# Store order of a mixture-of-experts stage: first and second picks alternate from quad to quad

## The reference

```python
h = gelu(ri @ r1_w.T + r1_b); probs = softmax(h @ r2_w.T)        # ri: the token and five statistics of it
topp, topi = top_k(probs, 2)                                     # each token picks two experts
score = where(routed, probs, -inf)
idx = argsort(-score, axis=0)[:cap].T                            # each of 32 experts takes its best 160 tokens
xe = xf[idx]
hact = silu(gate) * upv                                          # from xe @ w_up[e]
ye = hact @ w_down[e]
out = zeros((T, C)).at[idx.reshape(-1)].add(w * ye)              # the scatter-add: a token gets 0, 1 or 2 addends
out = out + sum_g gw * adapter_g(xf)                             # 16 small adapters, each shared by two experts
x = x + 0.5 * out
```

## Time and profile before

| | us |
|---|---|
| median of 3 runs | 1718.28 (1717.09 to 1720.53) |
| the profiled execution, its own time | 1708.64 |
| its span, first to last instruction | 1706.9 |
| first dispatch, POOL's first gather to its last store landed | 780.7 to 1101.5 |
| second dispatch, the same | 1385.5 to 1706.9 |
| mean granted TensorE clock | 0.905 of full speed |

### The profile page before, as it was taken

How to read it: one execution, slowest core, us unless ns; L and a number is a source line. 1 busy time by engine, 2 the same in 40 slices (tenths; PEclk the granted TensorE clock), 3 DMA queues, 4 the chain that set the end, 5 groups by cost and what they waited for, 6 DMA issues and landing times. The chain is left out here.

```text
span 1706.9 us, 26203 instructions
## 1 busy us (share of the span) xinstructions
PE 1427.4 (84%) x9328; PEld 1073.3 (63%) x9328; DVE 986.2 (58%) x2856; ACT 690.4 (40%) x1640; POOL 560.4 (33%) x465
## 2 busy tenths in 40 slices
PE   6899889999999678546999999299995459999994
PEld 5567545565555455335988999176663349888993
DVE  8787777787876479685552212057766855521110
ACT  4222137666666467443522332013333425323221
POOL 6522210000000154124254754332211232637644
PEclk9989889999999989656999999689997569999997
DMA  3035463423220013413687996421113326879983
GB/s 109 19 118 151 115 123 67 91 37 87 47 55 3 1 62 113 159 37 108 212 233 226 241 316 169 77 92 50 41 47 113 109 63 198 268 211 261 265 230 41
DMA packets 113483, 211.95 MB, mean 124 GB/s; under 512 B 20069, under 2 KB 79370, under 8 KB 104138
## 3 DMA queue, kind: packets, MB, share of 16 engines
q1 hardware_dynamic: 87338, 178.93, 32.7%
q0 software_dynamic: 26016, 31.34, 11.8%
HBM read 158.71 MB, written 51.12 MB: 123 GB/s over the span
## 5 line engine op out<-in xcount | busy, mean ns | idle before, releaser
L952 DVE TENSOR_REDUCE attnm_top<-psum 128x1 f32<-128x384 f32 (+3 forms) x384 | 212.9, 598 | 59.0 <-PE psum L1037 54.9
L1174 ACT ACTIVATE attnm_prob<-psum 128x512 f32<-128x512 f32 (+1 forms) x384 | 192.1, 530 | 88.9 <-PE psum L1047 82.3
L2553 DVE SCALAR_TENSOR_TENSOR moe2e_h<-moe2e_gate,psum 128x160 f32<-128x160 f32 x160 | 50.6, 321 | 187.2 <-ACT moe2e_gate L2491 187.1
L2553 DVE SCALAR_TENSOR_TENSOR moe1e_h<-moe1e_gate,psum 128x160 f32<-128x160 f32 x160 | 50.6, 321 | 186.3 <-ACT moe1e_gate L2491 186.2
L2356 POOL DMA_INDIRECT out<-moe2e_y,moe_scatter_i x74 | 116.4, 1573 | 113.8 <-DMA out<-moe2e_y,moe_scatter_i 58.4
L2356 POOL DMA_INDIRECT x_sum<-moe1e_y,moe_scatter_i x74 | 115.6, 1562 | 112.3 <-DMA x_sum<-moe1e_y,moe_scatter_i 65.9
L2425 PE MATMUL psum<-moe1e_xgT,moe_w_up 128*128 128x160 f32 x1024 | 149.5, 304 | 0.8 <-issue 0.8
L2425 PE MATMUL psum<-moe2e_xgT,moe_w_up 128*128 128x160 f32 x1024 | 149.4, 303 | 0.8 <-issue 0.8
L2425 PEld LDWEIGHTS psum<-moe1e_xgT,moe_w_up 128*128 128x128 f32 x1024 | 144.5, 193 | 3.5 <-issue 2.5
L2425 PEld LDWEIGHTS psum<-moe2e_xgT,moe_w_up 128*128 128x128 f32 x1024 | 144.3, 193 | 3.4 <-issue 2.5
L1348 POOL DMA_INDIRECT moe_xg<-xn_rows,moe_gather_i x80 | 83.4, 1043 | 155.0 <-DVE moe_gather_i L1537 93.0
(11 more groups left out here) (420 smaller groups left out, 3100.7 us busy)
## 6 DMA issues: line engine op xcount, KB each, us to landing
moe_w_up<-in_expert_up SPq DMA_DIRECT2D x64, 1024.0 KB, 8.4
moe_w_down<-in_expert_down SPq DMA_DIRECT2D x64, 512.0 KB, 6.9
attnm_q_hat<-q_parts SPq DMA_DIRECT2D x72, 128.0 KB, 4.6
moe_a_up<-in_adapter_up SPq DMA_DIRECT2D x32, 256.0 KB, 9.4
q_parts<-attnf_q_part SPq DMA_DIRECT2D x12, 512.0 KB, 2.8
attnm_k_hat<-k_parts SPq DMA_DIRECT2D x72, 64.0 KB, 2.3
x_res<-in_x SPq DMA_DIRECT2D x8, 512.0 KB, 8.9
v_tails<-attnf_v_tail SPq DMA_DIRECT2D x4, 1024.0 KB, 5.3
```

Source lines behind the costliest of these rows:

```text
L952: nc.vector.tensor_reduce(top[:, n // QUADS % 2, tiles[0]:tiles[-1] + 1, hh:hh + 1], s.ps[:, u.bank, 0:len(tiles) * width].rearrange("p (t ...
L1174: nc.scalar.activation(prob[:, i % NPROB, at:GROUP], s.ps[:, u.bank, at:GROUP], ACT.Exp).then_inc(taken[u.bank], 1)
L2553: nc.vector.scalar_tensor_tensor(out=h[:, HELD[n], i, :], in0=gate[:, i, :], scalar=1.0 if i < INTER // P else SCALE_A, in1=s.ps[:, u.bank ...
```

## The change

1. The waits of the stores are split: `y_out` becomes four semaphores, one for each parity of the quad and each list.
2. Quads 0 to 5: an even quad stores its first list and then its second, an odd quad the second and then the first. So the list that a quad begins with is the one that the quad before ended with, and as no token has two second picks (or two first ones), these may be in flight together. The wait for the quad before, and the return of its `y` buffer, move from ahead of the quad's first store to behind its third. The tail is stored ahead of tile 3.
3. Quads 6 and 7 are written out as six phases with a wait behind each. `whole` and `of_any` go.
4. The spare rows are doubled, so that neighbouring quads don't share any: `spare_no` is made by two iotas and a copy of 40 columns instead of 5, and the output has 640 more rows.

Gathers, loads and the order of all other engines stay.

```diff
--- before.py
+++ after.py
@@ -1203,7 +1203,7 @@
 ST_TILES = EQ * CAP // P
 SLOT_TILES = SLOTS // P
 ROW = C + 16
-SPARE = ST_TILES * P
+SPARE = 2 * ST_TILES * P
 QUADS_E = EXPERTS // EQ
 VALUES = 2
 HALF = EXPERTS // 2
@@ -1247,8 +1247,12 @@
             chain.link(nc.gpsimd.iota(ints[:, at:at + n], pattern, base=base, channel_multiplier=step))
             chain.link(nc.gpsimd.tensor_copy(out[:], ints[:, at:at + n]))
             at += n
-        chain.link(nc.gpsimd.iota(ints[:, at:at + ST_TILES], [[P, ST_TILES]], base=TOKENS + 1, channel_multiplier=1))
-        chain.link(nc.gpsimd.tensor_copy(s.spare_no[:], ints[:, at:at + ST_TILES]))
+        many = QUADS_E // 2 * 2 * ST_TILES
+        for n in range(QUADS_E // 4):
+            first = n * many // (QUADS_E // 4)
+            chain.link(nc.gpsimd.iota(ints[:, first:first + 4 * ST_TILES], [[ST_TILES * P, 2], [0, 2], [P, ST_TILES]], base=TOKENS + 1,
+                                      channel_multiplier=1))
+        chain.link(nc.gpsimd.tensor_copy(s.spare_no[:], ints[:, 0:many]))
         chain.link(nc.gpsimd.tensor_copy(self.mine[:, 0:HALF], s.ident[:, 0:HALF]))
         for j in range(1, PARTS):
             chain.link(nc.gpsimd.tensor_tensor(self.mine[:, 0:HALF], self.mine[:, 0:HALF], s.ident[:, HALF * j:HALF * (j + 1)], ALU.add))
@@ -1290,7 +1294,7 @@
     s.e_down = sb("e_down", [P, EXPERTS], F32)
     s.tile_no = sb("tile_no", [P, 2 * TILES], F32)
     s.row_no = sb("row_no", [P, 1], F32)
-    s.spare_no = sb("spare_no", [P, ST_TILES], F32)
+    s.spare_no = sb("spare_no", [P, QUADS_E // 2 * 2 * ST_TILES], F32)
     s.same_e = sb("same_e", [P, P], F32)
     s.before_e = sb("before_e", [P, P], F32)
     s.same_b = sb("same_b", [P, P], BF16)
@@ -1391,7 +1395,6 @@
         self.held = sb("held", [P, VALUES, self.tiles])
         self.token = sb("token", [P, self.tiles])
         self.added, self.spare = (sb(n, [P, self.quads, 2, ST_TILES]) for n in ("added", "spare"))
-        self.of_any, self.whole = sb("of_any", [P, self.quads, ST_TILES]), sb("whole", [P, self.quads, ST_TILES], I32)
         (self.scored, self.score_turned, self.score_copied, self.halved, self.high_made, self.low_made, self.tried, self.parted,
          self.counted, self.signed, self.totaled, self.tied, self.offset, self.placed, self.place_turned, self.pos_made,
          self.valued, self.hot_made, self.slotted, self.copied, self.listed, self.rows_known, self.slots_made, self.dve) = (
@@ -1538,15 +1541,9 @@
         nc.vector.tensor_scalar(first, second, -1.0, 1.0, ALU.mult, ALU.add)
         chain.link(nc.vector.tensor_tensor(added[:, :, 1], of_quad, second, ALU.mult))
         chain.link(nc.vector.tensor_tensor(added[:, :, 0], of_quad, added[:, :, 1], ALU.subtract))
-        spare_no = s.spare_no[:].rearrange("p (o k) -> p o k", o=1).broadcast_to([P, self.quads, ST_TILES])
-        chain.link(nc.vector.scalar_tensor_tensor(out=self.of_any[:], in0=of_quad, scalar=0.0, in1=spare_no,
-                                                  op0=ALU.is_equal, op1=ALU.mult))
-        nc.vector.scalar_tensor_tensor(out=self.whole[:], in0=of_quad, scalar=-1.0, in1=self.of_any[:],
-                                       op0=ALU.add, op1=ALU.add)
-        spare_no = s.spare_no[:].rearrange("p (o k) -> p o k", o=1).broadcast_to([P, 2 * self.quads, ST_TILES])
         chain.link(nc.vector.scalar_tensor_tensor(
-            out=spare[:].rearrange("p q i k -> p (q i) k"), in0=added[:].rearrange("p q i k -> p (q i) k"), scalar=0.0,
-            in1=spare_no, op0=ALU.is_equal, op1=ALU.mult))
+            out=spare[:].rearrange("p q i k -> p (q i k)"), in0=added[:].rearrange("p q i k -> p (q i k)"), scalar=0.0,
+            in1=s.spare_no[:], op0=ALU.is_equal, op1=ALU.mult))
         nc.vector.scalar_tensor_tensor(
             out=scatter_i, in0=added[:].rearrange("p q i k -> p (q i k)"), scalar=-1.0,
             in1=spare[:].rearrange("p q i k -> p (q i k)"), op0=ALU.add, op1=ALU.add).then_inc(self.slots_made, 1)
@@ -2217,7 +2214,7 @@
     gate = sb("gate", [P, PAIRS, CAP])
     HELD = [0, 1, 2, 3, 4, 0, 1, 2]
     h = sb("h", [P, EQ + 1, PAIRS, CAP])
-    y_out = sem("y_out")
+    y_out = [[sem(f"y_out{q}_{i}") for i in range(2)] for q in range(2)]
     y_free = [sem(f"y_free{q}") for q in range(2)]
     silu, chosen, weighed = sem("silu"), sem("chosen"), sem("weighed")
     banks = Banks(st)
@@ -2339,61 +2336,56 @@
                 pool.wait_ge(chosen, quad - 1)
             m.gather(pool, quad)
 
-        stored = itertools.count(1)
-
-        def add(quad):
-
+        stored = collections.Counter()
+
+        def store(quad, i, tiles):
 
             q, t = quad % 2, quad // 2
-            choice, at = m.choices[quad // late.quads], quad % late.quads
-            whole = [choice.whole[:, at, k:k + 1] for k in range(EQ)]
-            first, second = ([scatter_i[:, (quad * 2 + i) * ST_TILES + k:(quad * 2 + i) * ST_TILES + k + 1]
-                              for k in range(ST_TILES)] for i in range(2))
-
-            def store(k, rows):
+            for k in tiles:
                 u = u_tails[q] if k == TAIL else u_down[EQ * q + k]
+                at = (quad * 2 + i) * ST_TILES + k
                 pool.wait_ge(taken[u.bank], u.after(t))
-                nc.gpsimd.indirect_dma_start(total, bass.IndirectOffsetOnAxis(ap=rows, axis=0),
+                nc.gpsimd.indirect_dma_start(total, bass.IndirectOffsetOnAxis(ap=scatter_i[:, at:at + 1], axis=0),
                                              y[:, q, k, :], None, bounds_check=TOKENS + SPARE - 1, oob_is_err=True,
-                                             compute_op=ALU.add).then_inc(y_out, 16)
-                return next(stored)
-
-            def landed(n):
-                if n > 0:
-                    pool.wait_ge(y_out, 16 * n)
-
-            done = add.done
-            landed(done)
-            if quad > 0:
-                pool.sem_inc(y_free[1 - q], 1)
-            if quad < QUADS_E - 1:
-                for rows in (first, second):
-                    for k in range(ST_TILES):
-                        done = store(k, rows[k])
-                    if rows is first:
-                        landed(done)
-            else:
-                for k in range(EQ - 1):
-                    done = store(k, whole[k])
-                    landed(done)
-                for rows in (first, second):
-                    for k in (TAIL, EQ - 1):
-                        done = store(k, rows[k])
-                    if rows is first:
-                        landed(done)
-            add.done = done
-
-        add.done = 0
+                                             compute_op=ALU.add).then_inc(y_out[q][i], 16)
+                stored[q, i] += 1
+
+        def landed(quad, i):
+            pool.wait_ge(y_out[quad % 2][i], 16 * stored[quad % 2, i])
+
         gather(1)
         late.lows(pool)
         pool.wait_ge(x_kept, 16 * GROUPS)
-        for quad in range(QUADS_E):
+        for quad in range(QUADS_E - 2):
+            one, other = (0, 1) if quad % 2 == 0 else (1, 0)
             if quad + 2 == QUADS_E // 2:
                 pool.wait_ge(late.slots_made, 1)
-            if quad + 2 < QUADS_E:
-                gather(quad + 2)
-            add(quad)
-        pool.wait_ge(y_out, 16 * add.done)
+            gather(quad + 2)
+            store(quad, one, range(EQ - 1))
+            if quad > 0:
+                landed(quad - 1, one)
+                pool.sem_inc(y_free[1 - quad % 2], 1)
+            store(quad, one, (TAIL, EQ - 1))
+            landed(quad, one)
+            store(quad, other, range(ST_TILES))
+
+        a, b = QUADS_E - 2, QUADS_E - 1
+        store(a, 0, (0, 1))
+        landed(a - 1, 0)
+        pool.sem_inc(y_free[1], 1)
+        landed(a, 0)
+        store(a, 1, (0, 1))
+        landed(a, 1)
+        store(a, 0, (2, TAIL, 3))
+        landed(a, 0)
+        store(a, 1, (2, TAIL, 3))
+        store(b, 1, (0, 1))
+        landed(a, 1)
+        landed(b, 1)
+        store(b, 0, (0, 1, 2, TAIL, 3))
+        landed(b, 0)
+        store(b, 1, (2, TAIL, 3))
+        landed(b, 1)
 
     def tensor(pe):
         def turn_x(t, q, i):
```

## The result

The changed kernel took 1705.24 us (median of 4 runs, 1701.92 to 1708.93) against 1719.32 us for the kernel before (4 runs, 1717.09 to 1720.53): a ratio of 0.9915 [0.9889, 0.9940], 14.1 us less. The forecast was 1708.3, in 1702.5 to 1714.0. Two later sets of runs, on two chips, gave 1696.37 against 1709.01 (0.9927 [0.9905, 0.9948]) and 1696.27 against 1706.77 (0.9941 [0.9923, 0.9960]), so 12.6 and 10.5 us less.

The account below looks back on a forecast made before the run. POOL's stores and landing waits behind PE's last result were taken to bound the end. Savings of 5.15 + 4.8 us in the two dispatches, 10.0 together, off the median 1718.28 gave 1708.3 us, range 1702.5 to 1714.

Parts of the forecast that it names:

- What bounds the kernel: Behind PE's last result, POOL's stores and landings set the end: tails of 24.6 and 25.4 us can shorten.
- The sum of the tail: From quad 5's last store to the last store: 35.7 us of stores plus 18.6 of waits, 54.3.
- w1: Landing wait behind quad 6's first two stores, two stores after quad 5's five: 4.4 us, from 2.9 to 6.85.
- w2: Landing wait behind the second phase's two stores, issued as the down loads go out: 4.7 us, from 2.9 to 7.6.
- w3: Landing wait behind the third phase's three stores, issued as the loads end: 3.5 us, from 2.9 to 6.9.
- w4: Landing wait behind the fourth phase's five stores, on idle DMA engines: 3.0 us.
- w5: Landing wait behind the fifth phase's five stores, on idle DMA engines: 3.0 us.
- the forecast's own signs: Profile signs: bursts of 2, 2, 3, 5, 5, 3, waits near 4.4, 4.7, 3.5, 3.0, 3.0, last landing 5 us closer to PE's end.
- Small phases land as if idle: Rival in the tail: two-store phases slip in ahead of the loads, saving 7.5 + 0.5 per dispatch, 1702 us; chance 0.18.
- The second phase waits out the whole down load: Rival in the tail: its two stores land only after the loads, wait 11.9 us, 3.4 lost, 1721.7 us; chance 0.10.
- Quads 0 to 5: Savings on POOL ahead of the tail, from one wait and the lists: 0.5 us per dispatch, bounds 0 and 0.7.
- The later buffer return: `y_free` comes 5.6 us later, taken as 0; rival: ACT's stalls reach PE, half the saving goes, 1713 us; chance 0.12.

Follow-up runs that it names:

- the alternation alone: Against the kernel before: alternating list order with later buffer return in quads 0 to 6, last quad stored as before; 1704.2 us, ratio 0.9964.
- the two experiments on it: Against the changed kernel: buffer return ahead of the quad's first stores (1699.74 us), or behind all five stores of its first list (1698.51 us).

## Why the prediction was right

**What bounds the kernel**: right. The gain is on POOL, behind PE's last result; that result did not move but for the first profile (294.2 to 297.3 in the later two, 294.8 to 297.1 in the two of before), and the last landing came closer to it.

**The sum of the tail**: right in its total. Over the three profiles of the change, six tails, the means are

| | w1 | w2 | w3 | w4 | w5 | tail |
|---|---|---|---|---|---|---|
| forecast | 4.4 | 4.7 | 3.5 | 3.0 | 3.0 | 54.3 |
| measured, mean of six | 3.9 | 4.6 | 4.3 | 3.1 | 3.0 | 54.7 |
| lowest to highest | 2.7–4.7 | 2.9–7.5 | 2.9–8.6 | 2.9–4.0 | 2.8–3.1 | 52.0–58.5 |

against 59.1 for the four tails before (58.95, 58.62, 59.05, 59.71). That is 4.3 saved per dispatch, 5.1 without the late D2 of the first profile; forecast were 4.65 and 4.3. The single waits scatter more than the sum: w3 was 8.63 once for a forecast of 3.5, so by the forecast's own signs the first profile agrees in D1 and not in D2. The 2.0 + bytes/436 GB/s of the Trainium skill (DMA: Bandwidth & Descriptors, "Anatomy of one DMA — SWDGE (gpsimd) path"), an estimate of 2.3 us for a store, was set aside for the rows' 3.0 behind the issue. That was right: w4 and w5, counted from the end of the last issue, came to 2.8 to 3.1 in eleven of their twelve places.

**w2 by itself**: the mean of 4.6 against the forecast's 4.7 is luck. The 4.7 was taken from the gathers' median of 4.6, but that one covers all 80 gathers and not those among these loads, and it counts from the start of the issue, where w2 counts from the end of the last. And the forecast had one value for all executions. Measured, w2 goes from 3.0 to 7.5 as the lead falls from 3.8 to 2.0 us, and the lead varies by that much from dispatch to dispatch. Both rivals describe a part of it. *Small phases land as if idle* (w2 = 3.0) holds at the leads of 3.8 and 9.6. *The second phase waits out the whole down load* holds in its mechanism at leads of 2.0 and less, once in the change's six tails and in three of the variants'; its price was too high. It took the 11.9 from the landing before, 13.0 us behind the first load's issue, where five stores and the loads share the DMA engines; with two stores it is 8.8 to 9.3 and w2 at most 7.6. So its condition, w1 + w2 + w3 above 17.6, was never met (16.06 in the worst tail, the first profile's D2; 1.06 more with its wait for data). When the loads come late, phase 3 takes phase 2's place: 8.63, 5.05. The rule of the Trainium skill (same page, "Queues, rings and completion order"), that an increment lands only after every earlier write of its DMA engine, agrees with the trace at the short leads, where the landing came with the end of the loads (8.8 to 9.3 us behind their issue); no run separates it from a plain sharing of the engines.

**Quads 0 to 5**: forecast 0.5 per dispatch (0 to 0.7). Their last store ends at 256.5 to 257.7 in the two later profiles of the change and at 257.1 to 259.4 in the two of before, 1.0 apart in the mean, which is no more than the scatter; the alternation alone shows 258.4 and 259.5. Between nothing and 2 us in all, so the term was not off by much, and no experiment resolves it.

**The later buffer return**: taken as 0, rightly, but for a wrong reason. The forecast let the return come 5.6 us later, stall ACT by 1.2 us at quad 4, and be covered by PE's slack. The return that quad 4 needs did not move (166.8 us behind the first gather against 166.9), and ACT had it 2.8 us early. No profile has the wait of ACT for POOL that this rival needs; the two experiments on it moved this return too little to test it.

**The total**: 10.0 us forecast; 14.1, 12.6 and 10.5 measured in three sets. The two later sets agree with the profiles: from a dispatch's first gather to its last store, the four of the later profiles of the change take 311.3 in the mean and the four of before 317.3, so 6.0 per dispatch, 12.0 in all, of which 10.0 in the tails. The first set's 14.1 may hold some of its own scatter: with a standard deviation of 3 us, medians of four are uncertain by almost 2 each. The doubled spare rows are in every variant, so no run shows what they alone do; the landings on idle DMA engines mostly take 2.8 to 3.1 with and without them.

**What stays open**: the "remote" waits of the first profile. One of them, on ACT in D1, from its timeline:

```profile
1010.76 0.47 ACT L2503 ACTIVATE moe1e_y<-psum,moe1e_weight 128x256 f32<-128x256 f32 x1 [4.34 <-remote]
...
1014.43 0.47 ACT L2503 ACTIVATE moe1e_y<-psum,moe1e_weight 128x256 f32<-128x256 f32 x1 [2.28 <-remote]
```

PE's matmuls that write these tiles are recorded as done by about 1008.2 and 1010.9 (the profile models these ends), so the release reached ACT late by 2 to 4 us, and PE's work behind it shifted. The buffer return is not what they wait for: most of these rows are tails and gates, which don't need it (only the `weigh` of tile 0 does), and the one at quad 4's tile 0, 952.76, had its buffer at 949.4. They came in one of 13 profiles, and the same kernel twice didn't show them; so the change does not always bring them, and no run says what did.

## What to carry to other kernels

- A wait for a landing costs least where something independent can be issued into it. Splitting the stores by what may collide, and phasing the last two quads, took 4 to 5 us off each tail; moving three gathers in each dispatch into waits that POOL sat out anyway took 14 more off the kernel, and the profile of before already had the idle time beside the gathers.
- Stores issued just ahead of a large load are cheap only with enough of a head start: here 3.8 us, for two stores that POOL needs 3.4 us to issue. With 2.0 they landed only as the loads ended, 7.5 us behind the last issue and not 3.0. Read the order of issue on both queues, not only which transfer was first.
- Where a semaphore increment stands in the code is not when it happens: POOL's went out with the first of three stores that stand ahead of it. Look up its own row before pricing a moved one.
- Compare a span of waits with itself in several executions rather than two single profiles: here the profiled executions showed no gain at all where the medians showed 14 us.

## What the runs showed that was not expected

- The landing time's steep dependence on the lead, 3.0 to 7.5 us within 2 us of lead (table above).
- The buffer return that quad 4 needs didn't move with its place in the code.
- The gathers inside the waits gave 14.4 us, more than was expected of them. Of the 9 to 10 us by which quad 5's stores end earlier per dispatch, 6.5 in the mean are left at the last store, twice.
- Executions of one kernel on one chip differ by up to 14 us (1700.86 to 1715.34 in 23), and its medians in four sets, the last three each on another chip, are 1719.32, 1709.34, 1709.01 and 1706.77: only differences within a set can be read.
